# The input stage of a graph network kernel: x in four transfers, Wq and Q by quarters, edge products between Q and K

## The chip, the core and the metric

The kernel runs on one core of a Trainium2 chip. The core has a matrix engine (TensorE, PE in the profile; PEld is its weight load), VectorE (DVE), ScalarE (ACT), GpSimd (POOL) and SyncE (SP), which run their own lists of instructions and meet by semaphores. Matrix products write to eight banks of PSUM, `pb[0]` to `pb[7]`. Sixteen DMA engines move data; here SyncE and ScalarE issue the transfers, each on a queue of its own. The metric is the time of one execution in microseconds (us) on the device; the lower the better.

## What is computed

The input is a matrix x of 512 nodes by 512 features, 16384 edges, and the weights of two layers. Cut to what matters:

```python
xn = layernorm(x)                                   # only where the layer asks for it
q, k, v = xn @ Wq + bq, xn @ Wk + bk, xn @ Wv + bv  # 8 heads of 64, 32 graphs of 16 nodes
attn = q . k * 64 ** -0.5                           # inside a graph
attn[graph, src, dst] += edge_attr @ We + be        # edge products
x = x + softmax(attn) @ v @ Wo + bo
x = x + mixture_of_experts_0(layernorm(x))          # 8 experts, the best 2 of each node
x = chebyshev_graph_convolution(layernorm(x), src, dst, edge_weight) + ...
out = x + mixture_of_experts_1(layernorm(x))
```

The change is in the first stage alone: from the loads to the start of V.

## The kernel before

All of it is written by hand in one function, `build_network`: each engine has its list, in program order, and waits where a semaphore says so. There is no scheduler. Products are made in three parts: a float32 matrix is split into a high float16 half (ScalarE: scale and convert) and a low half (VectorE: value minus the high half), and `mm3` multiplies high by high, high by low and low by high, each a 128x128 by 128x512 product. So nothing on TensorE starts before both halves are there.

The stages, in order: the input stage (layer norm, transposes of x, Q, K, edge products, V, scores), a scatter of the edges by products with one-hot matrices, attention and its projection, the first experts, the Chebyshev stage, and the second experts. The experts' weights stream in through `r_stage`.

The input stage engine by engine:

- SyncE (lines 480 to 488) issues x as one transfer of 1 MB, then the three edge lists (`src_i`, `dst_i`, `w_f`), then Wq, the edge attributes (`attr`, and `we_b`), Wk, Wv, Wo, and then the first expert chunks (line 499).
- ScalarE (lines 671 to 680) issues fifteen small transfers: biases, router weights, and last `down_bias` and `b2` (`b_out`). Then `qkvo_hi_part(0)` makes the high half of all of Wq (line 705), `x_hi(0)` that of the turned x, in four parts from banks 4 to 7 (line 686), and then come Wk, Wv and Wo. `qk_out` (line 711) takes Q and K out of PSUM with their bias.
- VectorE takes the row statistics when x is there (lines 929, 930), GpSimd makes the reciprocal root (line 601), VectorE makes the normalized `xn` (line 948), then the low half of Wq (`qkvo_lo_part(0)`, line 970), the low half of the turned x (`x_lo(0)`, line 954), the edge indices (lines 980 to 990), the reading of the turned bias rows (lines 994 to 1003) and of the turned edge rows (1009 to 1016), the low half of Wk, and so on. At line 1041 it reads the edge products, and makes the operands of the scatter from line 1087 on.
- TensorE (from line 1606) runs 16 products of zeros (`keep_busy`, line 1603) into bank 3, the 16 transposes of x (`transpose_x(0)`, line 1592), again 16 products of zeros, and waits in `x_split(0)` for all halves of x. Q goes block by block: for each of four column blocks `c` the four `k` are summed, into banks 4 to 7. After two blocks the bias rows and the edge rows are transposed (`rows_turn`, `edges_turn`, into banks 0, 1 and 2). Then K into banks 0 to 3, behind `rows_read` and `base_ready`; then the edge products (line 1650) into banks 6 and 7, behind the four Q outputs of ScalarE (`qk_ready`); then V, the scores (line 1674), zeroed sums (line 1725) and the scatter (lines 1689 to 1691).

## Time and profile before

| What | us |
|---|---|
| median of 3 runs | 750.85 |
| lowest and highest | 749.01 and 751.69 |
| the profiled execution | 752.92 |
| its span in the profile | 751.1 |
| TensorE busy in it | 699.5 (93%) |
| VectorE busy | 584.1 (78%) |
| ScalarE busy | 385.0 (51%) |

The span is what the profiler sees between the first and the last instruction; the 1.8 us beside it belong to the execution's time. All positions below are us from the span's start. The granted clock of TensorE is 1.00 for 2.4 GHz and 0.50 for 1.2 GHz. "issue" stands for time in which an engine waited for nothing that the profile shows. Releasers are inferred, so a wait for several semaphores can stand under one of them. Matmul rows that follow each other overlap: their distance, not their length, is what one costs.

### The profile page before, as it was taken

To read this page: it belongs to the slowest core of one execution; us is meant where nothing else is said; L and a number is where in the kernel's file an instruction comes from. 1 tells how busy PE (TensorE), PEld (TensorE's weight loads), DVE (VectorE), ACT (ScalarE), POOL (GpSimd) and SP (SyncE) were. 2 spreads that over 40 slices of the span, in tenths; PEclk is the share of its full clock that TensorE was granted. 3 is DMA by queue.
4 is the path that set the end of the run, shared out by engine and by line. 5 is a ranking of instruction groups with operands and counts; after the bars stand their busy time and mean duration, and the time that the engine had idled before them with its cause. 6 is when DMAs were issued, how large, how long until landed. Compare 5 with 4: busy or idle time off the path is not lost.

```text
span 751.1 us, 22793 instructions
## 1 busy us (share of the span) xinstructions
PE 699.5 (93%) x8378; PEld 566.7 (75%) x8378; DVE 584.1 (78%) x1326; ACT 385.0 (51%) x684; POOL 115.2 (15%) x161
## 2 busy tenths in 40 slices
PE   6998999978789999999888999999789999999995
PEld 3457999934589999999873444444488999999993
DVE  4779999567898898888984764535788888888885
ACT  2442000033467777777754422220377888878882
POOL 2000000001000323123221000000010344443432
PEclk9999999999999999999996999999799999999998
DMA  9600111102169888899837430000247888989884
GB/s 302 252 1 3 46 45 44 45 2 74 44 231 332 309 268 321 291 329 301 247 129 235 152 105 1 1 0 1 74 143 240 262 246 279 268 268 284 275 251 130
DMA packets 38527, 128.31 MB, mean 171 GB/s; under 512 B 5488, under 2 KB 6080, under 8 KB 38320
## 3 DMA queue, kind: packets, MB, share of 16 engines
q1 hardware_dynamic: 32832, 120.44, 46.6%
q0 software_dynamic: 3264, 5.57, 5.0%
q10 hardware_dynamic: 2352, 1.23, 0.7%
q8 instruction: 52, 0.85, 0.5%
q14 instruction: 27, 0.22, 0.1%
HBM read 117.85 MB, written 9.37 MB: 169 GB/s over the span
## 4 chain that ended last, share of the span: by engine, by line
PE 60%; DVE 17%; DMA 9%; issue 8%; ACT 4%; POOL 1%; DVEq 1%; SPq 0%; ACTq 0%; POOLq 0%
PE pb L1583 11%; PE pb L1584 10%; PE pb L1585 10%; DMA r_stage<-in_chunks 8%; PE pb L1691 7%; DVE r_split L966 4%; PE pb L1814 4%; ACT r_split L702 3%; PE pb L1845 2%; PE pb L1847 2%; PE pb L1846 2%; PE pb L1689 2%; PE pb L1690 2%; DVE r_work L1409 2%; DVE r_work L1341 1%
## 5 line engine op out<-in xcount | busy, mean ns | idle before, releaser
L966 DVE SCALAR_TENSOR_TENSOR r_split<-r_stage,r_split 128x1024 f16<-128x1024 f32 (+1 forms) x160 | 230.6, 1443 | 44.8 <-ACT r_split L702 44.0
L702 ACT ACTIVATE r_split<-r_stage 128x1024 f16<-128x1024 f32 (+1 forms) x160 | 197.2, 1236 | 48.2 <-PE pb L1847 24.7
L1583 PE MATMUL pb<-r_work,r_split 128*128 128x160 f16 x864 | 183.0, 233 | 8.9 <-DVE r_work L1421 6.7
L1585 PE MATMUL pb<-r_work,r_split 128*128 128x160 f16 x864 | 183.0, 233 | 0.0
L1584 PE MATMUL pb<-r_work,r_split 128*128 128x160 f16 x864 | 183.0, 233 | 0.0
L1845 PE MATMUL pb<-r_work,r_split 128*128 128x160 f16 x608 | 130.8, 234 | 7.1 <-issue 3.6
L1847 PE MATMUL pb<-r_work,r_split 128*128 128x160 f16 x608 | 130.9, 234 | 0.0
L1846 PE MATMUL pb<-r_work,r_split 128*128 128x160 f16 x608 | 130.8, 234 | 0.0
L1583 PEld LDWEIGHTS pb<-r_work,r_split 128*128 128x128 f16 x864 | 84.5, 98 | 11.3 <-issue 6.6
L1691 PE MATMUL pb<-r_work 128*128 128x256 f16 x512 | 86.3, 274 | 0.0
L1690 PE MATMUL pb<-r_work 128*128 128x64 f16 x512 | 86.2, 194 | 0.0
L1689 PE MATMUL pb<-r_work 128*128 128x64 f16 x512 | 86.2, 193 | 0.0
L1584 PEld LDWEIGHTS pb<-r_work,r_split 128*128 128x128 f16 x864 | 84.5, 98 | 0.2
L1585 PEld LDWEIGHTS pb<-r_work,r_split 128*128 128x128 f16 x864 | 84.5, 98 | 0.0
L640 POOL DMA_INDIRECT x_dram<-r_work,rows_i x17 | 52.1, 3066 | 192.2 <-DVE r_work L1383 188.4
L1845 PEld LDWEIGHTS pb<-r_work,r_split 128*128 128x128 f16 x608 | 59.8, 98 | 8.5 <-issue 7.5
L1847 PEld LDWEIGHTS pb<-r_work,r_split 128*128 128x128 f16 x608 | 59.8, 98 | 0.0
L1846 PEld LDWEIGHTS pb<-r_work,r_split 128*128 128x128 f16 x608 | 59.8, 98 | 0.0
L1814 PE MATMUL pb<-r_work,r_mid 128*128 128x160 f16 x672 | 53.6, 233 | 3.0 <-DVE r_work L1341 3.0
L785 ACT ACTIVATE r_work<-r_work 128x160 f16<-128x160 f32 x152 | 50.3, 331 | 9.3 <-DVE r_work L1421 7.4
L1690 PEld LDWEIGHTS pb<-r_work 128*128 128x128 f16 x512 | 50.1, 98 | 6.2
L1689 PEld LDWEIGHTS pb<-r_work 128*128 128x128 f16 x512 | 50.4, 99 | 0.1
(294 smaller groups left out, 1264.4 us busy)
## 6 DMA issues: line engine op xcount, KB each, us to landing
r_stage<-in_chunks SPq DMA_DIRECT2D x68, 768.0 KB, 5.3
r_stage<-in_chunks SPq DMA_DIRECT2D x92, 512.0 KB, 4.7
r_gnn<-in_cheb_lin SPq DMA_DIRECT2D x3, 1024.0 KB, 9.4
r_split<-in_cheb_lin SPq DMA_DIRECT2D x3, 1024.0 KB, 14.7
x_dram<-x_sb SPq DMA_DIRECT2D x10, 256.0 KB, 2.6
x_sb<-x_dram SPq DMA_DIRECT2D x8, 256.0 KB, 3.5
x_sb<-in_x SPq DMA_DIRECT2D x1, 1024.0 KB, 5.8
r_split<-in_Wq SPq DMA_DIRECT2D x1, 1024.0 KB, 9.5
```

Source lines behind the costliest of these rows:

```text
L702: nc.scalar.activation(x.hi(c), x.stage(c), ACT.Copy, scale=W_SCALE).then_inc(x.whi, 1)
L966: V.scalar_tensor_tensor(x.lo(c), x.stage(c), W_SCALE, x.hi(c), ALU.mult, ALU.subtract)\
L1583: MM(o, sh, mh, start=start, stop=False)
L1584: MM(o, sh, ml, start=False, stop=False)
L1585: return MM(o, sl, mh, start=False, stop=stop)
L1689: MM(pb[t][:, cols], w, hi[:, c, 0:n], start=False, stop=False, skip_group_check=True)
L1690: MM(pb[t][:, cols], w, lo[:, c, 0:n], start=False, stop=False, skip_group_check=True)
L1691: last = MM(pb[6 + t // 2][:, 256 * (t % 2):256 * (t % 2) + 256], w, ebd_b[:, c, :, :].rearrange("p s q -> p (s q)"), start=False, stop=False,
L1814: last = MM(pb[4 + 2 * part + k // 2][:, o:o + S], src[:, t, k * P:(k + 1) * P], to_slot[:, t, :], start=t == 0, stop=t == T - 1)
L1845: MM(o, wh, ah_b[j % 4], start=j == 0 and d % 2 == 0, stop=False, skip_group_check=True)
L1846: MM(o, wh, al_b[j % 4], start=False, stop=False, skip_group_check=True)
L1847: last = MM(o, wl, ah_b[j % 4], start=False, stop=j == J - 1, skip_group_check=True)
```

## The change

x comes in four transfers of 128 rows each, with a semaphore for each, and VectorE takes the statistics of a part when it has landed. The three edge lists are issued behind Wq. ScalarE issues `down_bias` and `b2` after its parts of x, on a semaphore of their own (`bias_in`), and runs one activation on an unused tile ahead of its first wait. Wq still comes in one transfer, but its halves are made in four parts of 128x512, in turn with the parts of x, on both engines. The products of zeros are 10 ahead of the transposes and none behind them.

Q is summed over banks 0 to 3 at once: for each `k`, as soon as that part of Wq and x is there, the products of all four column blocks. The bias and edge rows are transposed after the third `k`, into banks 4 to 6. The edge products go between Q and K and wait for the reading of the bias rows (`rows_read`) in place of Q's outputs; K goes to banks 4 to 7, and its third and fourth blocks wait until VectorE has read the edge products from banks 6 and 7 (`eb_read`). For that, this reading moves ahead of the low half of Wv in VectorE's list. V waits for the outputs of Q where it waited for those of K. The remaining edits carry the new bank numbers and semaphore counts (`qw_hi` and `qw_lo` now count four for Wq).

```diff
-            sp.dma_start(x_sb[:, :, :], a["x"].rearrange("(t p) d -> p t d", p=P)).then_inc(x_in, 16)
-            for dst, name in ((src_i, "src"), (dst_i, "dst"), (w_f, "edge_weight")):
-                sp.dma_start(dst, a[name].rearrange("(c p) -> c p", p=P)).then_inc(edges_in, 16)
+            for t in range(T):
+                sp.dma_start(x_sb[:, t, :], a["x"][t * P:(t + 1) * P, :]).then_inc(x_in[t], 16)
             for m, name in enumerate(("Wq", "Wk", "Wv", "Wo")):
                 sp.dma_start(w_raw[m].rearrange("p (k n) -> p k n", k=K),
                              a[name].rearrange("(k p) n -> p k n", p=P)).then_inc(wraw_in[m], 16)
                 if m == 0:
+                    for dst, edge in ((src_i, "src"), (dst_i, "dst"), (w_f, "edge_weight")):
+                        sp.dma_start(dst, a[edge].rearrange("(c p) -> c p", p=P)).then_inc(edges_in, 16)
                     sp.dma_start(attr, a["attr"]).then_inc(attr_in, 16)
                     sp.dma_start(we_b, a["WeB"]).then_inc(attr_in, 16)
...
-            for f, name in enumerate(("down_bias", "b2")):
-                act.dma_start(b_out[f], a[name]).then_inc(small_in, 16)
-
-            def x_hi(n):
-
-                for k in range(K):
+            act.wait_ge(tables, 9)
+            nc.scalar.activation(unused[:, :], neg_half[:, :], ACT.Copy)
+
+            def x_hi(n, a=0, b=K):
+
+                for k in range(a, b):
...
-            qkvo_hi_part(0)
-            x_hi(0)
+            def wq_hi(k):
+                nc.scalar.activation(qkvo_hi[0][:, k, :], w_raw[0].rearrange("p (k n) -> p k n", k=K)[:, k, :], ACT.Copy,
+                                     scale=W_SCALE).then_inc(qw_hi, 1)
+
+            act.wait_ge(wraw_in[0], 16)
+            wq_hi(0)
+            wq_hi(1)
+            x_hi(0, 0, 1)
+            wq_hi(2)
+            x_hi(0, 1, 2)
+            wq_hi(3)
+            x_hi(0, 2, K)
+            for f, name in enumerate(("down_bias", "b2")):
+                act.dma_start(b_out[f], a[name]).then_inc(bias_in, 16)
...
-            dve.wait_ge(x_in, 16)
-            layernorm(0, xn)
-            qkvo_lo_part(0)
-            x_lo(0)
+            def wq_lo(k):
+                dve.wait_ge(qw_hi, k + 1)
+                V.scalar_tensor_tensor(qkvo_lo[0][:, k, :], w_raw[0].rearrange("p (k n) -> p k n", k=K)[:, k, :],
+                                       W_SCALE, qkvo_hi[0][:, k, :], ALU.mult, ALU.subtract).then_inc(qw_lo, 1)
+
+            for t in range(T - 1):
+                dve.wait_ge(x_in[t], 16)
+                ch.add(V.bn_stats(stats[:, t, :], x_sb[:, t, :]))
+            dve.wait_ge(x_in[T - 1], 16)
+            layernorm(0, xn, done=T - 1)
+            wq_lo(0)
+            wq_lo(1)
+            x_lo(0, 0, 1)
+            wq_lo(2)
+            x_lo(0, 1, 2)
+            wq_lo(3)
+            x_lo(0, 2, K)
...
             ch.link(V.tensor_copy(dl_h[:, :], dst_i))
+            ch.link(V.tensor_scalar(be_bc, be_bc, EB_SCALE, None, ALU.mult))
+            dve.wait_ge(eb_psum, 1)
+            half = C // 2
+            for i in range(2):
+                V.scalar_tensor_tensor(eb_f[:, half * i:half * (i + 1), :],
+                                       pb[6 + i][:, :].rearrange("p (c h) -> p c h", h=H), EB_SCALE,
+                                       bc(be_bc, 1, half), ALU.mult, ALU.add).then_inc(eb_read, 1)
             qkvo_lo_part(2)
...
-            ch.link(V.tensor_scalar(be_bc, be_bc, EB_SCALE, None, ALU.mult))
-
-            dve.wait_ge(eb_psum, 1)
-            half = C // 2
-            for i in range(2):
-                ins = V.scalar_tensor_tensor(eb_f[:, half * i:half * (i + 1), :],
-                                             pb[6 + i][:, :].rearrange("p (c h) -> p c h", h=H), EB_SCALE,
-                                             bc(be_bc, 1, half), ALU.mult, ALU.add)
-                (ch.add if i == 0 else ch.link)(ins)
+
+            dve.wait_ge(eb_read, 2)
...
-            keep_busy(3, 16)
+            keep_busy(3, 10)
             transpose_x(0)
-            keep_busy(3, 16)
...
             def rows_turn():
-                pe.wait_ge(small_in, 16 * 15)
+                pe.wait_ge(small_in, 16 * 13)
+                pe.wait_ge(bias_in, 32)
...
-            x_split(0)
-            for m in range(2):
-                pe.wait_ge(qw_hi, m + 1)
-                pe.wait_ge(qw_lo, m + 1)
-                if m == 1:
-                    pe.wait_ge(rows_read, 1)
-                    pe.wait_ge(base_ready, 1)
+            for k in range(K):
+                pe.wait_ge(qw_hi, k + 1)
+                pe.wait_ge(qw_lo, k + 1)
+                pe.wait_ge(xhi_ready, k + 1)
+                pe.wait_ge(xlo_ready, k + 1)
                 for c in range(K):
-                    for k in range(K):
-                        at = slice(c * P, (c + 1) * P)
-                        last = mm3(pb[4 * (1 - m) + c][:, :], qkvo_hi[m][:, k, at], qkvo_lo[m][:, k, at],
-                                   xT_hi[:, k, :], xT_lo[:, k, :], k == 0, k == K - 1)
-                    last.then_inc(qk_psum, 1)
-                    if m == 0 and c == 1:
-                        rows_turn()
-                        edges_turn()
+                    at = slice(c * P, (c + 1) * P)
+                    last = mm3(pb[c][:, :], qkvo_hi[0][:, k, at], qkvo_lo[0][:, k, at], xT_hi[:, k, :],
+                               xT_lo[:, k, :], k == 0, k == K - 1)
+                    if k == K - 1:
+                        last.then_inc(qk_psum, 1)
+                if k == 2:
+                    rows_turn()
+                    edges_turn()
 
             pe.wait_ge(attr_in, 32)
-            pe.wait_ge(qk_ready, K)
+            pe.wait_ge(rows_read, 1)
             for g in range(C // EC):
                 last = MM(pb[6 + g // 8][:, (g % 8) * EC * H:(g % 8 + 1) * EC * H], attr[:, g, :], we_b,
                           start=True, stop=True)
             last.then_inc(eb_psum, 1)
 
+            pe.wait_ge(qw_hi, K + 1)
+            pe.wait_ge(qw_lo, K + 1)
+            pe.wait_ge(base_ready, 1)
+            for c in range(K):
+                if c >= 2:
+                    pe.wait_ge(eb_read, c - 1)
+                at = slice(c * P, (c + 1) * P)
+                for k in range(K):
+                    last = mm3(pb[4 + c][:, :], qkvo_hi[1][:, k, at], qkvo_lo[1][:, k, at], xT_hi[:, k, :],
+                               xT_lo[:, k, :], k == 0, k == K - 1)
+                last.then_inc(qk_psum, 1)
+
             narrow = pe.value_load(flag_i[0:1, 0:1], min_val=0, max_val=1)
-            pe.wait_ge(qw_hi, 3)
-            pe.wait_ge(qw_lo, 3)
+            pe.wait_ge(qw_hi, K + 2)
+            pe.wait_ge(qw_lo, K + 2)
             for t in range(T):
-                pe.wait_ge(qk_ready, K + t + 1)
+                pe.wait_ge(qk_ready, t + 1)
                 at = slice(t * P, (t + 1) * P)
                 for k in range(K):
                     last = mm3(pb[t][:, :], xT_hi[:, k, at], xT_lo[:, k, at], qkvo_hi[2][:, k, :],
```

ScalarE's list behind its thirteenth transfer, before (`r_gnn<-r_split` of 128x2048 is the high half of one weight matrix, `r_xT` that of the turned x):

```order
L678 DMA rt_raw1<-in_WrT 128x4x8
L680 DMA r_mid<-in_down_bias 8x512
L680 DMA r_mid<-in_b2 8x512
L705 ACT_TABLE_LOAD
L705 ACTIVATE r_gnn<-r_split 128x2048 [waits wraw_in0]
L686 ACTIVATE r_xT<-pb4 128x512 [waits xt_psum]
L686 ACTIVATE r_xT<-pb5 128x512 [waits xt_psum]
L686 ACTIVATE r_xT<-pb6 128x512 [waits xt_psum]
L686 ACTIVATE r_xT<-pb7 128x512 [waits xt_psum]
L705 ACTIVATE r_gnn<-r_split 128x2048 [waits wraw_in1]
L705 ACTIVATE r_gnn<-r_split 128x2048 [waits wraw_in2]
```

and now:

```order
L682 DMA rt_raw1<-in_WrT 128x4x8
L684 ACT_TABLE_LOAD
L684 ACTIVATE unused<-neg_half 128x4 [waits tables]
L719 ACTIVATE r_gnn<-r_split 128x512 [waits wraw_in0]
L719 ACTIVATE r_gnn<-r_split 128x512
L690 ACTIVATE r_xT<-pb4 128x512 [waits xt_psum]
L719 ACTIVATE r_gnn<-r_split 128x512
L690 ACTIVATE r_xT<-pb5 128x512 [waits xt_psum]
L719 ACTIVATE r_gnn<-r_split 128x512
L690 ACTIVATE r_xT<-pb6 128x512 [waits xt_psum]
L690 ACTIVATE r_xT<-pb7 128x512 [waits xt_psum]
L731 DMA r_mid<-in_down_bias 8x512
```

The two bias loads have moved from ahead of the table load to behind the parts of x, and the high half of Wq (128x2048) has become four pieces of 128x512 between which the parts of x stand.

TensorE's list from the transposes of x to the first Q products, before (`pb3<-iota_n,zeros` is a product of zeros):

```order
L1592 MATMUL pb4<-ident,r_work 128x128 [waits xn_ready] x4
L1592 MATMUL pb5<-ident,r_work 128x128 [waits xn_ready] x4
L1592 MATMUL pb6<-ident,r_work 128x128 [waits xn_ready] x4
L1592 MATMUL pb7<-ident,r_work 128x128 [waits xn_ready] x4
L1603 MATMUL pb3<-iota_n,zeros 128x512 x16
L1583 MATMUL pb4<-r_xT,r_gnn 128x512 [waits qw_hi,qw_lo,xlo_ready,xhi_ready]
L1584 MATMUL pb4<-r_xT,r_gnn 128x512
L1585 MATMUL pb4<-r_xT,r_gnn 128x512
L1583 MATMUL pb4<-r_xT,r_gnn 128x512
```

and now:

```order
L1621 MATMUL pb4<-ident,r_work 128x128 [waits xn_ready] x4
L1621 MATMUL pb5<-ident,r_work 128x128 [waits xn_ready] x4
L1621 MATMUL pb6<-ident,r_work 128x128 [waits xn_ready] x4
L1621 MATMUL pb7<-ident,r_work 128x128 [waits xn_ready] x4
L1612 MATMUL pb0<-r_xT,r_gnn 128x512 [waits xhi_ready,xlo_ready,qw_lo,qw_hi]
L1613 MATMUL pb0<-r_xT,r_gnn 128x512
L1614 MATMUL pb0<-r_xT,r_gnn 128x512
L1612 MATMUL pb1<-r_xT,r_gnn 128x512
```

The sixteen products of zeros between the transposes and Q are gone, and the second group of three goes to another bank instead of being summed onto the first.

TensorE's list around the edge products (`pb6<-r_gnn,r_work`, 128x64), before, from the last product of K on:

```order
L1585 MATMUL pb3<-r_xT,r_gnn 128x512
L1650 MATMUL pb6<-r_gnn,r_work 128x64 [waits qk_ready,attr_in]
L1650 MATMUL pb6<-r_gnn,r_work 128x64 x7
L1650 MATMUL pb7<-r_gnn,r_work 128x64 x8
L1654 TENSOR_LOAD flag_i
L1654 ISA x2
L1583 MATMUL pb0<-r_gnn,r_xT 128x512 [waits qk_ready,qw_lo,qw_hi]
```

and now, from the last product of Q on:

```order
L1614 MATMUL pb3<-r_xT,r_gnn 128x512
L1677 MATMUL pb6<-r_gnn,r_work 128x64 [waits rows_read,attr_in]
L1677 MATMUL pb6<-r_gnn,r_work 128x64 x7
L1677 MATMUL pb7<-r_gnn,r_work 128x64 x8
L1612 MATMUL pb4<-r_xT,r_gnn 128x512 [waits base_ready,qw_lo,qw_hi]
```

The edge products stood between K and V and stand between Q and K; K's wait for both halves of Wk is now behind them.

## Rows read from the trace of the kernel before

**Rows 1.** The chain that ended last, early part: start, length in us, what
```profile
0.77 5.78 DMA x_sb<-in_x
...
6.58 1.88 DVE stats L929 x3
...
12.41 3.50 PE pb L1592 x14
15.91 3.50 PE pb L1603 x16
19.41 1.44 issue
...
43.30 3.52 PE pb L1650 x32
```

**Rows 2.** Stretches of TensorE: stretch, length, busy (count), granted clock, DMA share, GB/s
```profile
20.85:43.30 22.45, 22.45 (x114) 1.00 0.46 178
46.82:63.70 16.88, 14.87 (x313) 1.00 0.01 2
63.70:149.90 86.20, 86.20 (x1537) 1.00 0.12 40
```

**Rows 3.** Timeline of the queues and ScalarE: start, length, engine, line, what
```profile
3.02 0.60 SPq L484 DMA_DIRECT2D r_split<-in_Wq  x1
...
7.58 4.75 ACTq L680 DMA_DIRECT2D r_mid<-in_down_bias  x1
...
12.29 4.51 SPq L499 DMA_DIRECT2D r_stage<-in_chunks  x4
12.36 0.43 ACTq L680 DMA_DIRECT2D r_mid<-in_b  x1
...
12.82 1.28 ACT L705 ACT_TABLE_LOAD   x1 [12.82 <-issue]
```

**Rows 4.** Transfers issued in 0 to 30: KB, us from issue to landing
```profile
x_sb<-in_x SPq DMA_DIRECT2D x1, 1024.0 KB, 5.8
r_split<-in_Wq SPq DMA_DIRECT2D x1, 1024.0 KB, 9.5
r_work<-in_attr SPq DMA_DIRECT2D x1, 1024.0 KB, 11.2
...
r_gnn<-in_edge_weight SPq DMA_DIRECT2D x1, 64.0 KB, 5.1
```

**Rows 5.** Timeline of TensorE and VectorE in the input stage
```profile
4.01 6.10 PE L1603 MATMUL pb<-iota_n,zeros 128*128 128x512 f16 x16 [4.01 <-POOL slot_id L597]
...
11.50 4.41 PE L1592 MATMUL pb<-ident,r_work 128*128 128x128 f32 x16 [1.39 <-DVE r_work L948]
...
16.06 2.29 DVE L970 SCALAR_TENSOR_TENSOR r_gnn<-r_split,r_gnn 128x2048 f16<-128x2048 f32 x1 [3.24 <-ACT r_gnn L705]
18.27 2.48 DVE L954 SCALAR_TENSOR_TENSOR r_xT<-pb,r_xT 128x512 f16<-128x512 f32 x4
```

**Rows 6.** Groups by form, 380 to 520, splits of 128x512: busy, mean ns
```profile
L885 ACT ACTIVATE r_gnn<-r_split 128x512 f16<-128x512 f32 x12 | 6.5, 613 | 0.0
...
L1493 DVE SCALAR_TENSOR_TENSOR r_gnn<-r_gnn 128x512 f16<-128x512 f32 x12 | 7.6, 685 | 0.0
```

**Rows 7.** Two stretches: length, busy PE PEld DVE ACT POOL, clock, DMA, GB/s
```profile
12.00:13.00 1.00, 0.87 (x3) 0.39 (x4) 0.82 (x2) 0.18 (x1) 0.00 (x0) 0.73 1.02 419
15.00:16.00 1.00, 1.00 (x6) 0.80 (x5) 0.00 (x0) 1.00 (x2) 0.00 (x0) 0.56 1.09 366
```

**Rows 8.** Timeline of VectorE, four places, 26 to 55
```profile
27.06 0.17 DVE L994 COPY cols<-pb 128x8 f32<-128x8 f32 x1 [4.52 <-PE pb L1626]
...
29.61 2.27 DVE L970 SCALAR_TENSOR_TENSOR r_gnn<-r_split,r_gnn 128x2048 f16<-128x2048 f32 x1
...
46.93 1.29 DVE L1041 SCALAR_TENSOR_TENSOR r_mid<-pb,r_gnn 128x512 f32<-128x512 f32 x2 [3.80 <-PE pb L1650]
...
52.83 0.29 DVE L1087 TENSOR_TENSOR r_lap<-iota_n,r_lap 128x256 f16<-128x256 f16 x1 [1.03 <-issue]
```

51 lines of the change are left out of this document (27 added, 24 removed).

## Prediction, made before the changed kernel was run

> **What bounds the kernel now.** I read the chain of waits first, from its early end, and asked what starts TensorE. The reader is to see one series of hand-overs: x lands at 6.58 (0.77 + 5.78), VectorE takes the row statistics, TensorE turns x until 15.91, runs sixteen products of zeros, and then waits 1.44 until 20.85, where the first Q product starts [rows 1]. From there I looked only for gaps on TensorE: it is busy for all 22.45 us of 20.85 to 43.30 (Q, the small turns and K), then 3.52 of edge products follow [rows 1, 2]. V, the scores and the zeroing of the sums (46.82 to 63.70) have one gap of 2.01, which no other engine ends; 63.70 to 149.90 is the scatter, busy for 86.20 of 86.20 [rows 2]. So between 20.85 and 149.90 nothing but TensorE's own work sets the time. What the change is worth is how much earlier the first Q product starts, less what slows or stops TensorE behind it.
>
> Why 20.85: the queues tell. ScalarE issues its small loads itself, and the issue of down_bias holds it from 7.58 for 4.75 us, to 12.33; the last issue follows, and only at 12.82 comes the table load of 1.28 us [rows 3]. The split of Wq into a high and a low half then goes over whole matrices: VectorE's low half of Wq runs 16.06 to 18.35, and the four low parts of x from 18.27 for 2.48 us end at 20.75 [rows 5]. Wq itself had landed at 3.02 + 9.5 = 12.5 [rows 3, 4].
>
> **Part by part.** *x in four transfers.* VectorE's first three statistics (1.88 us, from 6.58 [rows 1]) go beside the transfers of the parts that follow; if the last quarter lands at 6.58 as the whole did, everything up to the turns is 1.88 earlier, and the turns end at 15.91 - 1.88 = 14.0. Four issues instead of one put the last at about 0.77 + 3 x 0.5 = 2.3 (issues of loads that are not held take 0.43 to 0.60 [rows 3]); a landing up to 1 us later would move the turns to 15.0 at most, and since the Q parts need the turned x one by one, that hardly moves the sum below.
>
> *Edge loads behind Wq.* The last of the three was issued one issue ahead of Wq, at about 2.55, and had landed 5.1 later, at 7.65, 1.07 after x [rows 3, 4]. Taken out from ahead of Wq they let it land up to 1.07 earlier: 11.45 at the low end, 12.5 at the high end (nothing gained, since ScalarE's small packets still share the engines). I take 11.9. Behind Wq they land near 13, and VectorE wants them after 17.
>
> *ScalarE's queue.* The two bias loads go behind the x parts, and an empty activation pulls the table load ahead. After the last issue ahead of 7.58 [rows 3], table load and dummy end near 9.0, so ScalarE waits for Wq: it starts its split at 11.9 rather than 14.1.
>
> *Wq and x in quarters.* The nearest 128x512 splits in SBUF cost 6.5 / 12 = 0.54 us a step on ScalarE, and 7.6 / 12 = 0.63 on VectorE [rows 6]. ScalarE: two Wq parts and the first x part end at 11.9 + 3 x 0.54 + 0.1 = 13.65. VectorE has its two Wq parts done by then and ends the first x part at 14.3, with 0.2 to 0.3 for hand-overs 14.6. Each later pass needs two more VectorE pieces, 1.25 us, and a pass is 12 products of 0.216 = 2.6 us (Q and K are 96 products, 20.75 of the 22.45 us [rows 2]; the other 1.7 are the turns of biases and edges). So only the first pass waits. Q starts at 14.6 instead of 20.85: **6.2 us**, between 5.6 (Wq at 12.5) and 6.7 (Wq at 11.45).
>
> *What TensorE meets behind it.* The bias and edge turns come after 36 products, at 14.6 + 7.8 = 22.4. The edge products (3.52) now stand ahead of K; they wait for the rows that VectorE reads after the turns and for nothing else that is late. K starts at 14.6 + 10.4 + 1.7 + 3.5 = 30.2. VectorE reads the rows from 22.4 + 1.0 = 23.4 and needs 2.55 (27.06 to 29.61 [rows 8]) and then 2.27 for the low half of Wk: 28.2, a cover of 2.0 us. If that cover is gone, K waits and all behind it. K's third bank waits for the first read of the edge products; VectorE gets to them near 30.3 and K's third bank is not due before 30.2 + 5.2 = 35.4. Wk, Wv and Wo land no earlier than before, but VectorE's demands for them stay later than that.
>
> *VectorE behind it.* Its list up to the first scatter operand (52.83) is the same with one change: it no longer sits 3.80 us before the edge read [rows 8]. So that operand comes at 25.95 + (52.83 - 29.61) - 3.80 = 45.4, 7.4 earlier, while TensorE's scatter starts 6.2 earlier. The operands keep their lead and the scatter stays TensorE's.
>
> *The clock.* This is the term I can bound but not place. Matmuls in 4.01 to 10.11 took 6.10 us for sixteen; the same sixteen from 15.91 took 3.50 [rows 1, 5]: most of the first ran at 1.2 GHz, the second at 2.4. The granted clock falls within 12 to 13, after TensorE had done little since 10.11, and is back within 15 to 16 [rows 7]; from means of 0.73 and 0.56 between the two levels of 1.0 and 0.5 it was low from 12.46 to 15.88. The change drops six zero products ahead of the turns and all sixteen behind them. If the clock is up when Q starts, and stays, the cost is 0. If one more stretch like that (3.4 us) falls on Q, the work in it takes twice as long: 1.7 us lost. Rows lean neither way: the wait of 1.44 us before Q did not lower it [rows 1, 2], a wait of 1.39 with sparse turns behind it did [rows 5, 7]. I take half, **0.8**.
>
> Sum: 6.2 - 0.8 = **5.4 us**. The profiled execution took 752.92 (span 751.1 and 1.8 around it) and would come to 747.5. It lies 2.1 above the median of the runs shown, 750.85, for which I forecast **745.4**. One engine sets the time in the changed part without a gap, so I expect no loss of it later. The stages after the scatter all start from its end.
>
> **Rivals.** *A: Q starts cold.* The turns do not bring the clock up, and Q runs at 1.2 GHz from its start. Price: a stretch as long as 3.4 us, or as the first 5 us of the kernel's own start, in which sixteen products took 6.10: 1.7 to 2.5 lost, so 6.2 - 2.5 gives 747.1. For it: all sixteen zero products that stood between turns and Q are gone. Against: when the clock rose at 15.88, the turns had run since 12.41 and ended at 15.91, so that at most one zero product had started [rows 1, 7]. The Trainium skill (TensorE: Matmul & The Clock Gate, Part 4: PE-mode transpose) says that transposes do not count as activity that raises the clock. By that rule this rival would hold; the trace speaks against it.
>
> *B: the bias rows come late.* TensorE waits for down_bias and b2 at 22.4. ScalarE issues them at about 16.2 and 16.7 and no row shows how long such a load takes while 16 engines are full: the edge loads took 5.1, attr, behind other transfers, 11.2 [rows 4]. At 5.1 they land at 21.8, in time. At 8 to 9 TensorE loses some 3 us: 748.5.
>
> *C: slower than before.* The same place, with the price of both rows: if the issue of down_bias is held 4.75 us again, and the load then takes 11.2, it lands at 16.2 + 4.75 + 0.5 + 11.2 = 32.6 and TensorE, due at 22.4, waits 10.2: 755.6. The change is slower once the load lands later than 27.8. Against: the issue of b2 at 12.36 took 0.43 us while SyncE's own issues of 12.29 took 4.51 for four, so one full queue does not hold the other [rows 3]; ScalarE's queue has had over 8 us to drain by 16.2.
>
> *D: given back.* Something in front of the scatter's end, such as K behind the low half of Wk if VectorE is 2 us later than I count, or the operands, takes most of the gain: 750.
>
> **How the numbers follow.** Forecast: 0.58, from 6.7 with no slow stretch to 5.6 with a whole one, 744.1 to 747.0. A: 0.20. B: 0.08. C: 0.05. D: 0.05. Better than the forecast, because Wq lands ahead of 11.45, with two small loads fewer beside it (742.8 to 744.1): 0.04. The range, 742.8 to 748.6, holds the forecast, the better case, A and half of B. Within 0.3% (2.25 us) is about what a measurement of this kernel can't tell from no change. Faster by over 0.3%, below 748.6: 0.58 + 0.20 + 0.04 + half of B = 0.86. Same: the other half of B and D, 0.09. Slower: C, 0.05.
>
> **What would show it.** In the changed kernel: ScalarE's table load ends before 10 and its first Wq part starts within 0.1 us of the landing; the first Q product starts at 14.6; between passes TensorE has no gap; the turns of the bias rows follow the third pass at once; the edge products end and K starts near 30.2; the first scatter product comes at 57.5. The granted clock from 12 to 20 decides between forecast and A, the wait of the bias turn between forecast, B and C. I am wrong if Wq lands after 12.5, or if K waits for VectorE by more than the 2.0 us counted.

## The result, and the profile after

The changed kernel takes 742.34 us in the median of 4 runs (739.53 to 746.11) against 750.37 (749.01 to 751.69, 4 runs) for the kernel before beside it: a ratio of 0.9886, with a 95% interval of 0.9848 to 0.9924. A second series of 6 runs gave 741.64 and a ratio of 0.9880 (0.9846 to 0.9913). The sign was forecast; the time was not: 742.3 lies 0.5 under the range, and the gain is 8 us where 5.4 were forecast.

The chain that ended last, early part of the changed kernel (start, length in us, what), to be set beside [rows 1]:

```profile
2.63 8.39 DMA r_split<-in_Wq
...
11.05 1.15 ACT r_gnn L719 x2
12.20 0.48 ACT r_xT L690
...
12.88 9.56 DMA r_mid<-in_b
22.45 0.14 issue
22.59 0.30 PE pb L1650
...
26.94 3.52 PE pb L1677 x32
```

Where x stood, Wq stands now. The chain no longer goes through the statistics and the transposes: the landing of Wq at 11.02 is what ScalarE waits for. The second DMA is `b2`: it was issued at 12.88, and the turn of the bias rows waited for it.

The timeline of the changed kernel shows the same by engine (start, length, engine, line, what, and in brackets the idle time ahead and what ended it), to be set beside [rows 3, 5]:

```profile
6.35 0.69 DVE L946 BATCH_NORM_STATS2 stats<-x_sb 128x6 f32<-128x512 f32 x1 [0.21 <-DMA x_sb<-in_x]
7.21 1.28 ACT L684 ACT_TABLE_LOAD   x1 [7.21 <-issue]
9.49 3.01 PE L1621 MATMUL pb<-ident,r_work 128*128 128x128 f32 x16 [1.03 <-DVE r_work L964]
...
11.05 1.15 ACT L719 ACTIVATE r_gnn<-r_split 128x512 f16<-128x512 f32 x2 [2.34 <-DMA r_split<-in_Wq]
...
13.75 0.38 PE L1612 MATMUL pb<-r_xT,r_gnn 128*128 128x512 f16 x1 [1.25 <-ACT r_xT L690]
...
22.59 0.30 PE L1650 MATMUL pb<-ident,r_mid 128*128 128x128 f32 x1 [0.90 <-DMA r_mid<-in_b]
```

The table load is done at 8.49, ScalarE is idle for 2.34 us and starts within 0.03 of the landing of Wq. The transposes take 3.01 us where they took 4.41. Q starts at 13.75 instead of 20.85. The last row is the only gap between 13.75 and the scores: 0.90 us for the bias rows.

The second place is the end of the scatter. The timeline of TensorE there, first of the kernel before:

```profile
149.64 0.27 PE L1691 MATMUL pb<-r_work 128*128 128x256 f16 x1
151.61 0.30 PE L1731 MATMUL pb<-iota_n,zeros 128*128 128x1 f16 x6 [1.70 <-issue]
151.78 3.40 PE L1603 MATMUL pb<-iota_n,zeros 128*128 128x512 f16 x15
```

and of the changed kernel:

```profile
145.31 0.27 PE L1730 MATMUL pb<-r_work 128*128 128x256 f16 x1
145.42 0.29 PE L1770 MATMUL pb<-iota_n,zeros 128*128 128x1 f16 x6
145.58 1.46 PE L1632 MATMUL pb<-iota_n,zeros 128*128 128x512 f16 x6
147.45 2.75 PE L1632 MATMUL pb<-iota_n,zeros 128*128 128x512 f16 x12 [0.42 <-issue]
```

The six products of one column close the sums of the scatter, and VectorE's attention work starts from them. Before, TensorE stood for 1.70 us, waiting for nothing that the profile shows, ahead of them. Now a stop of 0.42 comes six zero products behind them, where nobody waits. The next stage's first product follows 5.5 us behind the first closing product in both changed traces, in before_again and in zeros_only, so the 1.7 us are gained whole, in a stage that the change did not touch.

The third is the end of the first experts. TensorE's waits within 382 to 398, of the kernel before and of the changed one (engine, line, waited for: us in total, times, longest):

```profile
PE pb L1845 <- issue: 3.6, 1, 3.6
```

```profile
PE pb L1884 <- DVE r_work L1438: 2.6, 1, 2.6
```

It is the same product in both, one us less of a stop. Most of the stop is a plain wait, and only its end is not. The product needs the low half that VectorE makes (L1409 before, L1438 now), and the timelines show when that comes, of the kernel before and of the changed one:

```profile
391.92 0.30 DVE L1409 SCALAR_TENSOR_TENSOR r_work<-r_work 128x160 f16<-128x160 f32 x1
393.83 0.23 PE L1845 MATMUL pb<-r_work,r_split 128*128 128x160 f16 x1 [3.59 <-issue]
```

```profile
386.43 0.30 DVE L1438 SCALAR_TENSOR_TENSOR r_work<-r_work 128x160 f16<-128x160 f32 x1
387.30 0.23 PE L1884 MATMUL pb<-r_work,r_split 128*128 128x160 f16 x1 [2.56 <-DVE r_work L1438]
```

Some 2.0 us pass in both until the half is there (392.22 and 386.73); TensorE then takes 1.6 us more before and 0.6 us now.

Over both profiled runs of each kernel, the first scatter product comes at 63.5 and 62.6 before, 58.5 and 60.2 after; the last of the six closing products at 151.8 and 150.5 before, 145.6 and 146.5 after.

### The profile page after: what moved, and what is told of

It is laid out like the page before. It is cut to its first block, busy times and chain, and to the rows that moved or that the text cites. A ratio compares the mean times of both kernels' runs of the same rounds, so it can differ in the third digit from the quotient of the medians.

```text
span 744.3 us, 22765 instructions
## 1 busy us (share of the span) xinstructions
PE 696.0 (94%) x8356; PEld 564.6 (76%) x8356; DVE 584.6 (79%) x1329; ACT 384.7 (52%) x688; POOL 113.2 (15%) x161
## 4 chain that ended last, share of the span: by engine, by line
PE 65%; DVE 14%; DMA 9%; issue 6%; ACT 3%; POOL 2%; SPq 1%; DVEq 1%; ACTq 0%; POOLq 0%
PE pb L1612 11%; PE pb L1613 11%; PE pb L1614 11%; PE pb L1730 8%; PE pb L1853 5%; DMA r_stage<-in_chunks 4%; DVE r_split L982 3%; PE pb L1884 3%; PE pb L1886 3%; PE pb L1885 3%; PE pb L1728 2%; PE pb L1729 2%; DMA x_sb<-x_dram 2%; ACT r_split L706 2%; PE pb L1632 1%
```

## The experiments

A program's time goes with the mean granted clock of its run. Over all 168 timed runs of this study, a line through time against mean clock, with one level for each kernel, has a slope of -0.38 (+- 0.03) us for each 0.001 of clock and leaves 1.7 us of scatter in a single run. The kernel before has 65 runs in all, the changed one 10. The column "equal clock" is each kernel's level on it at 0.983; its uncertainty is one standard error. The column also credits a kernel with low clock that its own edit brings, and with low clock over idle time, where it costs nothing; where it and the ratio differ much, as in zeros_only and pad18, the text says so. Q, scatter and stops are from one profiled run each; the stops are the ones at the end of the scatter (S) and at about 390 us (E). "Scatter ends" is the start of the last closing product. A stop in brackets stands behind the closing products; "none" means that no idle time is listed there.

| kernel | median | ratio, 95% | equal clock | Q starts | scatter ends | S | E |
|---|---|---|---|---|---|---|---|
| before | 751.2 | | 751.0 +- 0.2 | 20.85 | 151.8 | 1.7 | 3.6 |
| before_again | 754.9 | | | 20.14 | 150.5 | 1.5 | 3.9 |
| after, after_again (ratio: second series) | 741.7 | 0.9880 (0.9846 to 0.9913) | 741.9 +- 0.6 | 13.75, 15.43 | 145.6, 146.5 | (0.4), (0.4) | 2.6, 2.5 |
| queue_only | 750.9 | 0.9983 (0.9959 to 1.0007) | 749.9 +- 0.5 | 19.48 | 149.8 | 1.5 | 3.5 |
| loads_queue | 747.1 | 0.9967 (0.9938 to 0.9996) | 748.3 +- 0.5 | 17.68 | 147.3 | 0.7 | 3.4 |
| zeros_only | 747.6 | 0.9957 (0.9935 to 0.9979) | 745.8 +- 0.6 | 20.59 | 150.4 | none | 2.6 |
| edge_products_late | 745.5 | 0.9933 (0.9907 to 0.9959) | 745.2 +- 0.5 | 13.54 | 147.8 | none | 2.8 |
| fill | 744.2 | 0.9920 (0.9892 to 0.9947) | 743.8 +- 0.6 | 15.3 | 146.1 | 1.7 | 2.4 |
| pad12 | 744.8 | 0.9907 (0.9882 to 0.9933) | 744.4 +- 0.7 | 15.32 | 146.6 | 1.8 | 2.2 |
| pad18 | 748.4 | 0.9932 (0.9903 to 0.9961) | 745.4 +- 0.5 | 15.13 | 148.0 | 1.7 | 3.6 |
| router_late | 742.4 | 0.9886 (0.9856 to 0.9915) | 742.3 +- 0.7 | 15.5 | 145.7 | (0.4) | 2.5 |
| no_turns | 741.2 | 0.9869 (0.9829 to 0.9910) | 743.0 +- 0.7 | 14.86 | 143.8 | (1.0) | 2.6 |
| wq_in_four | 740.8 | 0.9856 (0.9813 to 0.9899) | 740.9 +- 0.7 | 14.28 | 143.1 | (0.5) | 2.3 |

**The two kernels again.** No edit.

> The kernel before once more, for a second trace. In the first, TensorE stopped without another engine's doing ('issue') for 2.0 us in the scores, 1.7 at the end of the scatter, 1.9 before the router and 3.6 near 390; the changed kernel shows 2.0, 0.4 and 1.9. Theory F (a stop goes with a fixed place in TensorE's list, and its length with the work queued ahead of it): the stop at the end of the scatter is there again, between the last scatter product and the first closing product, 1 to 2 us. Rival: it was chance, and is gone or elsewhere. The 3.6 near 390 I expect to be chance.

> The changed kernel once more, in more rounds. Theory S (start): the gain is the earlier start of the first Q product (20.85 to 13.75 by the two traces, 7.1) less the 0.9 that TensorE then waits for the bias rows, 6.2 us, and whatever is beyond it comes from the granted clock of later stages, which differs from run to run. Then time against mean granted clock over the runs falls on one line, some 0.4 us for 0.001 of clock, and the gain at equal clock is 6 to 7 us. Rival L (later stage): the change itself gains 2 us more behind the input stage; then the gain at equal clock is 8 to 9 us.

Measured: the second traces give the ranges within which one kernel's own trace moves. Wq, issued at 2.63, landed 10.1 us later instead of 8.4, so Q started at 15.43, and TensorE never waited for the bias rows. TensorE's timeline of this second trace:

```profile
9.98 4.41 PE L1621 MATMUL pb<-ident,r_work 128*128 128x128 f32 x16 [1.51 <-DVE r_work L964]
15.43 0.59 PE L1612 MATMUL pb<-r_xT,r_gnn 128*128 128x512 f16 x1 [1.04 <-ACT r_xT L690]
15.80 0.63 PE L1613 MATMUL pb<-r_xT,r_gnn 128*128 128x512 f16 x1
16.23 0.63 PE L1614 MATMUL pb<-r_xT,r_gnn 128*128 128x512 f16 x1
...
19.22 0.55 PE L1612 MATMUL pb<-r_xT,r_gnn 128*128 128x512 f16 x1
19.60 0.38 PE L1613 MATMUL pb<-r_xT,r_gnn 128*128 128x512 f16 x1
19.82 0.38 PE L1614 MATMUL pb<-r_xT,r_gnn 128*128 128x512 f16 x1
```

The products stand 0.43 apart, twice the 0.22 of the first trace: ten products as at 1.2 GHz, 2 us lost. This is rival A, in one of two traces. The stops S and E came back as in the first trace, to 0.1 us.

**loads_queue**: the kernel before with the change's loads (x in four, edge lists behind Wq) and ScalarE's queue. Q, its order and the zero products as before.

```diff
-            sp.dma_start(x_sb[:, :, :], a["x"]...).then_inc(x_in, 16)
+            for t in range(T):
+                sp.dma_start(x_sb[:, t, :], a["x"][t * P:(t + 1) * P, :]).then_inc(x_in[t], 16)
...
+            act.wait_ge(tables, 9)
+            nc.scalar.activation(unused[:, :], neg_half[:, :], ACT.Copy)
```

> The kernel before with the loads and ScalarE's queue as changed (x in four, edge lists behind Wq, the two bias loads behind the parts of x, the empty activation), but Wq split whole, Q by column blocks, the products of zeros and the place of the edge products as before. Theory S: Wq lands near 11.0, its high half ends 13.0, its low half 15.2, the parts of x 17.8, so Q starts at 17.8 instead of 20.85: 3.0 us faster than before. The bias rows land near 22.5 and are due at 23.0: no wait. Rival Q: the quarters and the sum over four banks are the whole gain, and this one gains under 1.5 us.

Measured: Wq landed at 10.94, Q started at 17.68, 3.2 us earlier, and 2.7 us of time came of it at equal clock. What held Q was VectorE's low halves: 2.29 us for all of Wq, then four parts of x. Its stop S was 0.75 us, half of what the others with the long list show, and its place the same.

**queue_only**: the kernel before with the edit of ScalarE's queue alone.

```diff
-            for f, name in enumerate(("down_bias", "b2")):
-                act.dma_start(b_out[f], a[name]).then_inc(small_in, 16)
+            act.wait_ge(tables, 9)
+            nc.scalar.activation(unused[:, :], neg_half[:, :], ACT.Copy)
...
             x_hi(0)
+            for f, name in enumerate(("down_bias", "b2")):
+                act.dma_start(b_out[f], a[name]).then_inc(bias_in, 16)
```

> The kernel before with only the edit of ScalarE's own queue: the loads of the experts' bias rows go behind the splits of the input, and the table of the activation is loaded by an unused activation ahead. x, Wq, the order of Q and the zero products stay as they were. Theory: Wq lands at 12.5 as before, but ScalarE is free for its split by then instead of 14.1, so Q starts 1.6 us earlier, 19.2 instead of 20.85, and the time is 1.6 us shorter, 749.1 beside 750.7. loads_queue, which has x in four transfers on top, started Q at 17.7; the rest, 1.5 us, would be x's. Rival R (the statistics of x are late, not ScalarE): Q starts at 20 to 20.9 and the time is that of the kernel before within 0.7 us.

Measured: the theory's mechanism, at a little less. The timeline shows that ScalarE takes up Wq as it lands, and that VectorE ends last ahead of Q:

```profile
12.74 1.91 ACT L707 ACTIVATE r_gnn<-r_split 128x2048 f16<-128x2048 f32 x1 [4.01 <-DMA r_split<-in_Wq]
14.69 2.29 DVE L974 SCALAR_TENSOR_TENSOR r_gnn<-r_split,r_gnn 128x2048 f16<-128x2048 f32 x1 [1.99 <-ACT r_gnn L707]
16.90 2.48 DVE L958 SCALAR_TENSOR_TENSOR r_xT<-pb,r_xT 128x512 f16<-128x512 f32 x4
19.48 0.38 PE L1587 MATMUL pb<-r_xT,r_gnn 128*128 128x512 f16 x1 [1.63 <-issue]
```

16.90 + 2.48 = 19.38, and Q follows at 19.48, 0.7 to 1.4 ahead of the kernel before. The time is 1.1 (+- 0.6) shorter at equal clock; the interval of the ratio holds 1, so this part alone is not established. With loads_queue the way from 20.85 to 13.75 divides: 1.4 by the queue, 1.8 by the loads (Wq lands 1.8 earlier), 3.9 by the quarters.

**zeros_only**: the kernel before with only the zero products of the change, 22 products fewer.

```diff
-            keep_busy(3, 16)
+            keep_busy(3, 10)
             transpose_x(0)
-            keep_busy(3, 16)
```

> The kernel before with only the products of zeros changed: 10 instead of 16 ahead of the transposes and none instead of 16 behind them, 22 fewer. Q still starts near 20.85, since VectorE's parts of x set that. Theory F: the place of the stop lies 22 products later in the work, behind 6 closing products and 16 products of zeros, whose 3.5 us cover it: 1.7 us faster than before, less up to 1.7 if Q now runs at 1.2 GHz for a stretch. Theory S alone (only the start counts): same as before or up to 1.7 us slower.

Measured: the most telling run. Q started at 20.59, no earlier than in the kernel before within 0.5 us, and its first eight products stood 0.43 apart, so the early part lost some 1.8 us. Still the kernel is faster: by 3.2 us by the ratio (1.6 to 4.9), and by 5.2 (+- 0.6) at equal clock. The second number is too high for a gain in time: the mean clock of these runs is 0.976 beside 0.981, and in the trace the granted clock is low from about 10 to 24, over 4.8 us in which TensorE stands still anyway. In its trace the scatter takes 86.2 us instead of 88.1, with no stop ahead of the closing products, and the stop E is 2.6 instead of 3.6: 2.8 us at those two places. A third stop, at the scores, is 0.5 to 0.8 us shorter (below, at pad18). Less the 1.8 lost on Q the three make 1.5 to 1.8 us, at the low end of the ratio's interval; what the runs gained beyond that is not placed. So the zero products were not just a matter of the clock: where they stand in the list moves stops that come 40, 130 and 370 us later.

**edge_products_late**: the changed kernel with the edge products behind K again.

```diff
-            pe.wait_ge(attr_in, 32)
             pe.wait_ge(rows_read, 1)
-            for g in range(C // EC):
-                last = MM(pb[6 + g // 8][:, ...], attr[:, g, :], we_b, start=True, stop=True)
-            last.then_inc(eb_psum, 1)
...
+            pe.wait_ge(attr_in, 32)
+            pe.wait_ge(qk_ready, 2 * K)
+            for g in range(C // EC):
+                last = MM(pb[6 + g // 8][:, ...], attr[:, g, :], we_b, start=True, stop=True)
+            last.then_inc(eb_psum, 1)
```

> The changed kernel with the edge products behind K again, waiting for K's outputs, and read by VectorE where they were read before. Theory S: TensorE does the same work and waits once for ScalarE's last output of K, 0.7 to 0.9 us; VectorE waits about 3.8 us for the products but has that much lead: 1 us slower than the changed kernel. Rival V: VectorE's place decides, the scatter's operands come late, and it is 3 us or more slower than the changed kernel.

Measured: 3.3 us slower than the changed kernel at equal clock. TensorE's timeline, where it waits:

```profile
28.08 0.38 PE L1611 MATMUL pb<-r_xT,r_gnn 128*128 128x512 f16 x1 [1.78 <-DVE r_gnn L986]
...
39.47 3.76 PE L1688 MATMUL pb<-r_gnn,r_work 128*128 128x64 f32 x32 [0.87 <-ACT r_split L715]
```

K waits 1.78 for VectorE's low half of Wk, and the edge products 0.87 for ScalarE's output of K. Between Q and K the edge products cover the first wait and do not have the second: 2.65 of the 3.3 us. The cover of 2.0 us that the prediction counted is real and is used. (This trace has 0.5 us of wait for the bias rows as well; the changed kernel has 0.9.)

**fill**: the changed kernel with 12 zero products ahead of the transposes and 5 behind them, 7 more.

```diff
-            keep_busy(3, 10)
+            keep_busy(3, 12)
             transpose_x(0)
+            keep_busy(3, 5)
```

> The changed kernel with 12 instead of 10 products of zeros ahead of the transposes and 5 behind them, which fills TensorE's idle stretch of 12.5 to 13.75 without moving Q. Theory S with a warm Q in every run: the same time as the changed kernel within 0.5 us. Rival C (my term of 0.8 us): in some runs Q runs at 1.2 GHz for a stretch; then this one is 0.5 to 1.7 us faster in the median and its runs scatter less.

Measured: 1.9 (+- 0.8) slower than the changed kernel at equal clock. The scatter's end in its timeline:

```profile
144.13 0.27 PE L1771 MATMUL pb<-iota_n,zeros 128*128 128x1 f16 x5
146.14 0.16 PE L1771 MATMUL pb<-iota_n,zeros 128*128 128x1 f16 x1 [1.74 <-issue]
```

The stop is back, whole, and now stands between the fifth and the sixth closing product. That is odd for anything but a place in the list. Count TensorE's entries from the start of its list to the first closing product (two for each product, since its weights are an entry, one for each other instruction): 4526 before, 4488 in the changed kernel, 4502 in fill. The stop stands at 4502 + 10 = 4512 in fill, and at 4488 + 24 = 4512 in the changed kernel, behind six closing and six zero products. With 4526 entries, as before, that place falls inside the loop of `wide_scatter`, the other branch, which the list holds ahead of the closing products and which these runs jump over; the stop stands at the first entry behind it. Part of the 1.9 us is nearer: the halves for Q were there at 13.20, but the transposes ended at 14.4 and the five zero products followed, so that Q started at 15.30, some 1.1 us later than without them.

**pad12**: a test of that. The changed kernel with 12 products of eight columns behind the transposes. They take 0.5 us in all and bring the first closing product to entry 4512.

```diff
             transpose_x(0)
+            for _ in range(12):
+                MM(pb[3][:, 0:8], zeros[:, :], iota_n[:, 0:8], start=True, stop=True)
```

> The changed kernel with 12 products of 8 columns in TensorE's idle stretch behind the transposes (about 0.5 us, Q does not move). Theory F: the stop moves 12 products towards the front, from behind the sixth product of zeros to ahead of the closing products of the scatter, and is 1.3 us longer; the whole is 1.3 us slower than the changed kernel. Theory S alone: no difference.

Measured: a stop of 1.82 right ahead of the first closing product, where the count puts it:

```profile
146.44 0.29 PE L1772 MATMUL pb<-iota_n,zeros 128*128 128x1 f16 x6 [1.82 <-issue]
```

The kernel is 2.5 (+- 0.9) slower than the changed one at equal clock. The stop E did not grow.

**pad18**: the same with 18, so that the count is that of the kernel before within two entries, 4524.

```diff
             transpose_x(0)
+            for _ in range(18):
+                MM(pb[3][:, 0:8], zeros[:, :], iota_n[:, 0:8], start=True, stop=True)
```

> The changed kernel with 18 products of 8 columns more in TensorE's list, ahead of the first Q product, where it waits for the splits anyway (their own time is under 1 us and stands beside that wait). With them the list ahead of the closing products has again as many entries as in the kernel before. Theory F (the stops of TensorE at the end of the scatter and at about 390 us stand at a fixed count of the list from the last jump, and their length is some 1.8 and 3.6 us less the products that are queued ahead): with 18 more, the stop at the end of the scatter stands at or ahead of the first closing product, 1.5 to 1.8 us long instead of 0.42, and the one at about 390 is 2.2 to 3.6 long; 1.2 to 2.4 us slower than the changed kernel, 743.1 to 744.3 beside 741.9. Rival C (their lengths are chance, or go with the time at which they come): no change that the count explains, the time of the changed kernel within 0.7 us.

Measured: both stops are back, at the places and lengths of the kernel before. Timeline at the scatter's end, and waits within 382 to 398:

```profile
147.85 0.30 PE L1772 MATMUL pb<-iota_n,zeros 128*128 128x1 f16 x6 [1.71 <-issue]
```

```profile
PE pb L1886 <- issue: 3.6, 1, 3.6
```

3.5 (+- 0.8) us slower than the changed kernel at equal clock, more than the 1.2 to 2.4 of theory F and far from rival C; 6.8 in the medians, whose runs had the lower clock (0.979 beside 0.983). Some 0.5 us of it are the eighteen products themselves: they ran from 14.60 to 15.27, and Q's halves had been there at 14.00. Against the kernel before, which has the same stops S and E, pad18 is 5.6 (+- 0.6) us faster at equal clock, 5.1 by the ratio: that is the earlier start without the stops.

Over all fourteen traces E is 3.4 to 3.9 in the five with 4524 to 4527 entries ahead of the closing products, and 2.2 to 2.8 in the nine with 4512 or fewer. The wait for VectorE's half is 2.0 of it in all of them; behind that half the five stand 1.5 to 1.9 us more, the nine 0.2 to 0.8.

A third stop can be followed product by product, which rules out chance as its cause. In the scores, or right behind them, TensorE stands still in every trace for 1.2 to 2.3 us with no engine named. The timelines of the kernel before, the changed kernel, pad18 and zeros_only have it here:

```profile
61.85 0.46 PE L1674 MATMUL pb<-r_split 64*32 64x32 f32 x21 [2.01 <-issue]
```

```profile
56.08 0.25 PE L1713 MATMUL pb<-r_split 64*32 64x32 f32 x2 [2.01 <-issue]
```

```profile
56.56 0.65 PE L1715 MATMUL pb<-r_split 64*32 64x32 f32 x20 [2.27 <-issue]
```

```profile
63.02 1.25 PE L1724 MATMUL pb<-iota_n,zeros 128*128 128x512 f16 x5 [1.19 <-issue]
```

21 products of the scores follow the stop before, 2 in the changed kernel, whose list is 38 entries, 19 products, shorter up to there. With fill's 7 more products 9 follow it, with 12 more 14, with 18 more 20. With zeros_only's 22 fewer than before it stands one product behind the end of the scores, and is 1.19 us long. The other traces fit: 21 in before_again, 22 in queue_only and loads_queue, 3 in edge_products_late, 2 in the rest. So in all fourteen traces this stop stands at one entry of the list, to within one. In the change it moves by 19 products and keeps its length. One more view divides them in the same way, the profile's table of DMA queues (packets, MB, share). The kernel before (and, in packets and MB, before_again, queue_only, loads_queue and pad18):

```profile
q8 instruction: 52, 0.85, 0.5%
```

The changed kernel (and, in packets and MB, all the others):

```profile
q8 instruction: 51, 0.84, 0.5%
```

A queue of its own brings the instructions, and the five traces with the longer stop E have one packet more. That TensorE waits for its own list, at the stop in the scores, at S and at the end of E, fits all fourteen traces; no row names that wait, so the mechanism is inferred and the dependence on the count is what is shown. The length is not explained: the stop that stands behind six closing and six zero products is 0.4 us long in three traces and 1.0 in no_turns.

**router_late**: the changed kernel with the bias rows issued where they stood before, and the router's weights, which come in pieces of 32 bytes, issued behind the parts of x instead.

```diff
-            for f, name in enumerate(("router_w", "WrT")):
-                act.dma_start(rt_raw[f][:, :, :], ...).then_inc(small_in, 16)
+            for f, name in enumerate(("down_bias", "b2")):
+                act.dma_start(b_out[f], a[name]).then_inc(bias_in, 16)
...
-            for f, name in enumerate(("down_bias", "b2")):
-                act.dma_start(b_out[f], a[name]).then_inc(bias_in, 16)
+            for f, name in enumerate(("router_w", "WrT")):
+                act.dma_start(rt_raw[f][:, :, :], ...).then_inc(rt_in, 16)
```

> The changed kernel with the two router weights (1024 pieces of 32 bytes) issued behind the parts of x instead of ahead, on a semaphore of their own, and the two bias loads ahead in their place. If those pieces are what holds Wq and the bias rows up: Wq lands 0.5 to 1.5 us earlier than 11.0, TensorE does not wait for the bias rows (0.9 in the changed kernel), and it is 1.4 to 2.4 us faster than the changed kernel. If the amount of data alone counts (32 KB): only the 0.9 goes.

Measured: the time of the changed kernel. The small pieces do not hold Wq back: it landed 10.1 us after its issue, the later of the two landings seen. The bias wait is gone, as it is in after_again, where Wq was late too. What decides between 8 and 10 stays open: it was 8.2 to 8.4 in after, loads_queue, edge_products_late and no_turns, 7.9 in fill, 8.8 in pad18, 10.0 to 10.1 in after_again, pad12 and router_late, with the same loads ahead of it in most of them.

**no_turns**: the changed kernel with the splits in plain order.

```diff
-            wq_hi(0)
-            wq_hi(1)
-            x_hi(0, 0, 1)
-            wq_hi(2)
-            x_hi(0, 1, 2)
-            wq_hi(3)
-            x_hi(0, 2, K)
+            for k in range(K):
+                wq_hi(k)
+            x_hi(0)
```

and the same on VectorE.

> The changed kernel with ScalarE's and VectorE's splits in plain order: Wq's four quarters, then x's four, instead of in turn. Q's first product needs one quarter of each, so it now waits for all four of Wq and the first of x: Theory: Q starts some 1.3 to 1.7 us later behind Wq's landing, 4.0 to 4.4 instead of 2.7, and since the products of the first four passes wait for nothing else, the time is that much longer, 743.2 to 743.6 beside 741.9. Rival P (TensorE was held by the splits in turn, with short gaps in the passes, which the plain order does not have): the later start is given back before the turn, and the time is that of the changed kernel within 0.5 us.

Measured: the start is as the theory has it, 14.86 with Wq landed at 10.93, 3.9 behind the landing instead of 2.7. The total is inconclusive: 1.1 (+- 0.9) us slower at equal clock, and no slower in the medians.

**wq_in_four**: router_late with Wq in four transfers.

```diff
+            for k in range(K):
+                sp.dma_start(w_raw[0][:, k * D:(k + 1) * D], a["Wq"][k * P:(k + 1) * P, :]).then_inc(wq_in[k], 16)
...
             def wq_hi(k):
+                act.wait_ge(wq_in[k], 16)
```

> The changed kernel with Wq loaded in four transfers of 256 KB, one for each quarter, each with a wait of its own, and with the tiny loads behind it rearranged as in router_late (bias rows of the experts ahead, router weights behind the turn). In the changed kernel ScalarE takes up the first quarter only when all of Wq is there (11.0 or 12.7 us), and Q starts 2.7 us later. Theory L (that wait is the one that ends last ahead of Q): the first quarter lands some 2 us ahead of the last, ScalarE splits it then, and the splits of the others go with the loads; Q starts as soon as the last quarter has landed plus one split or so, 12.3 to 13, against 13.75 to 15.4; 1 to 2.5 us faster than the changed kernel, 739.5 to 741 beside 741.9. Rival M (the transposed x is late as well, or four transfers land later than one, since each has its own start): Q starts at 13.5 to 15 as before, and the time is that of the changed kernel within 0.5 us.

Measured: theory L for the load, rival M for the start. In its timeline ScalarE and TensorE read:

```profile
8.64 1.13 ACT L724 ACTIVATE r_gnn<-r_split 128x512 f16<-128x512 f32 x2
...
10.17 4.27 PE L1626 MATMUL pb<-ident,r_work 128*128 128x128 f32 x16 [2.19 <-DVE r_work L969]
...
12.05 0.60 ACT L694 ACTIVATE r_xT<-pb 128x512 f16<-128x512 f32 x1 [2.28 <-PE pb L1626]
...
14.28 0.38 PE L1617 MATMUL pb<-r_xT,r_gnn 128*128 128x512 f16 x1
```

Two quarters of Wq are split from 8.64 on, as soon as the table is loaded; now ScalarE waits 2.28 us for the turned x. The transposes ran at 1.2 GHz in this run, 4.27 us, and Q followed on their end at 14.28. So Wq is no longer what is late; x is. It is the fastest kernel of the study, 740.8 in the median and 740.9 at equal clock, 1.0 (+- 0.9) ahead of the changed one: probably better, not established. Against the kernel before its ratio is 0.9856.

## Why the prediction was wrong, point by point

**Right, and seen.** ScalarE's queue: table load done at 8.49 (9.0 said), first Wq part 0.03 us behind the landing. x's last quarter had landed by 6.35 (6.58 said). Passes without gaps. Edge products ahead of K, K without a wait; they end and K starts at 30.46 (30.2 said; that closeness is luck, since Q started 0.85 early and the bias rows then cost 0.90), and edge_products_late shows that the cover was needed. VectorE's first scatter operand came at 45.61 (45.4 said). The scatter stayed TensorE's.

**Q starts at 14.6.** 13.75 in the first trace, 15.43 in the second: the number lies between two landings of Wq, 11.02 and 12.69, of which it had taken the middle of its own range, 11.45 to 12.5. That range was too narrow at both ends.

**Rival B, the bias rows.** It came about in small: `b2` took 9.56 us to land, near the upper of the two rows that bounded it (5.1 and 11.2), but ScalarE issued it at 12.88 instead of 16.7, so that the wait was 0.90 us where B had 3. The issue did not hold ScalarE as down_bias had (0.38 us, against the 4.75 of [rows 3]), as the argument against C said. Where Wq is late the wait is gone.

**The clock.** 0.8 was taken, half of a slow stretch. The first trace lost nothing on Q, the second 2.0 us. In the profile's granted clock the second does not show (1.00 from 11 to 21, beside products 0.43 apart); in router_late and zeros_only the same distance stands beside a granted clock of 0.50, so distances between products are the better reading there. What goes with a cold Q is idle time behind cold transposes: in after_again, router_late and zeros_only TensorE stood still for 1.0 us or more between the two, and eight to ten products of Q ran at 1.2 GHz; in fill, wq_in_four and no_turns, where the transposes were as slow (4.3 to 4.4 us) and a product followed within 0.25 us, it was at 2.4 GHz at once. pad12 does not fit this: small products stood right behind its cold transposes, and the first three products of Q still ran at 1.2 GHz. In the first trace the transposes themselves ran at 2.4 GHz, and 1.25 us of idle time did not lower it. The Trainium skill (TensorE: Matmul & The Clock Gate, Part 4: PE-mode transpose) says that transposes do not count as activity that raises the clock. These three runs speak against it in that form, since transposes were all that TensorE had done in the 4 us ahead; after_again, where the products behind the transposes stayed slow, agrees with it, and so does zeros_only, where the granted clock was 0.50 from 12 to 20 with the transposes run from 11.35 to 15.76. What decides stays open. Rival A was worth more than the chance of 0.20, and in the mean of two traces the term of 0.8 was nearly right.

**The step that failed** is the last sentence of the sum: "One engine sets the time in the changed part without a gap, so I expect no loss of it later. The stages after the scatter all start from its end." It took the rest of the program as a block that only moves. And the dropped zero products were costed through the clock alone. They also shorten TensorE's list, and with that the stop S leaves the path (1.5 to 1.7 us) and the stop E gets 1.1 shorter: zeros_only takes both away with this edit alone, and pad12 and pad18 bring them back. The part that the prediction did work out was right in size: 5.4 forecast, 5.6 (+- 0.6) in pad18, which has the change and the old stops. The stop was there to be read, 1.70 of "issue" ahead of the closing products, as were the "issue" pieces of 1.44 and 2.01 that the prediction did name; it counted none of them as movable. The one row that contradicted "busy for 86.20 of 86.20" stood 0.01 us behind the stretch that was read. The lower end of the range, 742.8, came from no row: the earliest landing that was worked out gives 744.1.

**The balance.** The first scatter product was forecast at 57.5. It is 5.0 us earlier in the first trace (63.5 to 58.5, of which a slow stretch at 56.1 to 60.4, granted clock 0.60, took 0.9) and 2.4 to 3.4 in the second, which paid 2.0 for the clock. Take 5.2 for the start (63.05 before in the mean of both traces, 57.6 and 58.2 after with those two losses taken off), 1.7 for S and 1.1 for E: 8.0, against 8.0 in the medians of the first series and 9.1 (+- 0.6) at equal clock. The last us is open. One candidate is the second experts, from their first gather to the first weighting of their outputs on ScalarE: 193.2 to 195.7 us in the eight traces with 4502 entries or fewer, 194.9 to 196.9 in the six others. The ranges overlap, and no wait in them was found that goes with the count.

## What to carry to other kernels

Read each "issue" wait of the critical engine as a price that an edit can move: count the instructions that an edit adds to or takes from that engine's list, and expect 1 to 3 us either way at places that the edit does not touch. When the first of two inputs is made faster, say at once what the second one costs: here ScalarE waited 2.34 us for Wq in the changed kernel, and with Wq in four transfers it waited 2.28 us for the turned x. Products that only keep an engine busy are not free, even where they stand beside a wait: they lengthen the list, and in fill they held Q up themselves.

## What the runs showed of the hardware

Stops of TensorE stood at a fixed entry of its list, whatever stood there. The one in the scores did so in all fourteen traces, over a difference of 22 products (1.2 to 2.3 us long). The one at the scatter's end stood at entry 4512 in the changed kernel, router_late, no_turns, fill and pad12: 1.7 to 1.8 us long with closing products alone or nothing ahead of it (fill, pad12), 0.4 to 1.0 us where 1.3 us of queued zero products stood ahead of it. In the five traces where the engine jumped over that entry it came at the entry behind the jump, 0.75 to 1.7 us long.

A 1 MB load, issued at 2.63 behind the same loads, landed after 7.9 to 8.8 us in six traces and after 10.0 to 10.1 in three. A load of 16 KB on another queue, issued while the sixteen engines were full, took 9.56 us.

The time of a run follows its mean granted clock by 0.38 us for 0.001. Within a run the stretches at a low granted clock stood at other places from run to run: between the transposes and the scatter's start, near 160 to 190, 385 to 415 and 520 to 545, and from 729 on.
